# Two single-row blocks per turn instead of one in a GRU over gathered table rows: the second split between SyncE and ScalarE's queue, in a ring of 16 steps

## What is computed

```python
x = emb[item_seq]; mask = item_seq != 0          # 12,500 items x 128; sequences 512 x 200
def step(h, (x_t, m_t)):
    mx = x_t @ W + b_i
    mh = h @ U + b_r
    z = sigmoid(mx[:, :D] + mh[:, :D])
    r = sigmoid(mx[:, D:2*D] + mh[:, D:2*D])
    hh = tanh(mx[:, 2*D:] + r * mh[:, 2*D:])
    h_new = z * h + (1 - z) * hh
    return where(m_t, h_new, h)
out = softmax(h_last @ Wout + bout)
```

## Time and profile before

| what | value |
|---|---|
| median of 3 runs | 1039.23 us (1037.85 to 1040.12) |
| the profiled execution, its own time | 1038.45 us |
| its span, first to last instruction | 1036.5 us |
| busy share of the span | PE 94%, DVE 76%, POOL 74%, ACT 57% |
| granted TensorE clock, mean | 0.995 of full speed |
| DMA | 184.29 MB, mean 178 GB/s |
| chain that ended last | PE 55%, POOL 27%, "issue" 10%, DMA 3%, DVE 3%, ACT 1% |

### The profile page before, as it was taken

The page is one execution under the profiler, slowest core; times in us unless marked ns, Lnnn a source line. Parts: engine busy times, 40 slices in busy tenths (PEclk is TensorE's granted clock), DMA queues, the critical chain, the costliest instruction groups (busy, mean ns, idle before and its releaser), DMA issues.

```text
span 1036.5 us, 20050 instructions
## 1 busy us (share of the span) xinstructions
PE 976.5 (94%) x5218; PEld 760.8 (73%) x5218; DVE 792.0 (76%) x2075; ACT 593.2 (57%) x1301; POOL 765.7 (74%) x807
## 2 busy tenths in 40 slices
PE   6999999999999999999999999998898888988986
PEld 4556888777777777777777777776666666766765
DVE  3444667888888888888888888887777877777776
ACT  2334555666666666666666666655555555555555
POOL 5677777777777777777777777777777777777773
PEclk9999999999999999999999999999999999999999
DMA  9997555555555555555555555555555555555553
GB/s 356 403 373 279 150 161 159 161 161 160 163 158 161 163 157 161 161 161 161 159 163 158 161 160 161 160 160 162 157 161 163 157 160 161 159 161 159 164 163 95
DMA packets 62053, 184.29 MB, mean 178 GB/s; under 512 B 16428, under 2 KB 19812, under 8 KB 62020
## 3 DMA queue, kind: packets, MB, share of 16 engines
q0 software_dynamic: 48640, 147.77, 49.6%
q1 hardware_dynamic: 11984, 35.24, 8.9%
q10 hardware_dynamic: 1396, 0.91, 0.3%
HBM read 157.78 MB, written 26.07 MB: 177 GB/s over the span
## 4 chain that ended last, share of the span: by engine, by line
PE 55%; POOL 27%; issue 10%; DMA 3%; DVE 3%; ACT 1%; DVEq 0%; SPq 0%; POOLq 0%; ACTq 0%
POOL arena L359 27%; PE bank L453 14%; PE bank L459 9%; PE bank L455 9%; PE bank L441 8%; PE bank L375 5%; PE bank L447 4%; DMA rows<-turned 2%; PE bank L422 1%; PE bank L427 1%; PE bank L423 1%; DVE h L630 1%; ACT cand L561 1%; DVE rh L625 1%; PE bank L380 1%
## 5 line engine op out<-in xcount | busy, mean ns | idle before, releaser
L359 POOL DMA_INDIRECT arena<-table,row_table x734 | 694.7, 946 | 223.9 <-issue 218.7
L559 ACT ACTIVATE bank<-bank,b_gates 128x256 f32<-128x256 f32 x400 | 179.2, 448 | 252.2 <-PE bank L459 252.2
L441 PE MATMUL bank<-ident,arena 128*128 128x128 f32 x1496 | 249.8, 277 | 40.4 <-DMA arena<-table,row_table 39.5
L453 PE MATMUL bank<-h,U_sb 128*128 128x256 f32 x800 | 265.9, 414 | 1.7 <-DVE h L630 1.6
L640 DVE SCALAR_TENSOR_TENSOR bank<-bank,cand 128x256 f32<-128x256 f32 x400 | 172.7, 432 | 121.7 <-ACT cand L561 118.9
L441 PEld LDWEIGHTS bank<-ident,arena 128*128 128x128 f32 x1496 | 184.5, 141 | 106.0 <-DMA arena<-table,row_table 67.8
L561 ACT ACTIVATE cand<-pre,bi 128x256 f32<-128x256 f32 x400 | 202.9, 507 | 86.4 <-DVE pre L634 86.4
L459 PE MATMUL bank<-h,U_sb 128*128 128x256 f32 x800 | 240.3, 382 | 0.0
L625 DVE SCALAR_TENSOR_TENSOR rh<-bank,br,r 128x256 f32<-128x256 f32 x400 | 193.5, 484 | 58.2 <-ACT r L557 55.2
L455 PE MATMUL bank<-h,U_sb 128*128 128x256 f32 x800 | 237.9, 379 | 0.0
L557 ACT ACTIVATE r<-bank,b_gates 128x256 f32<-128x256 f32 x400 | 189.8, 475 | 34.2 <-PE bank L453 30.7
(11 more groups left out here) (61 smaller groups left out, 249.9 us busy)
## 6 DMA issues: line engine op xcount, KB each, us to landing
arena<-table SPq DMA_DIRECT2D x1792, 1.5 KB
table<-proj SPq DMA_DIRECT2D x24, 768.0 KB, 5.3
arena<-table,row_table POOLq DMA_INDIRECT x734, 3.1
arena<-in_L_rec_emb SPq DMA_DIRECT2D x12, 512.0 KB, 10.4
rows<-turned SPq DMA_DIRECT2D x12, 512.0 KB, 10.3
raw<-rows,row_table POOLq DMA_INDIRECT x52, 4.8
seq<-in_r_item_seq ACTq DMA_DIRECT2D x1, 400.0 KB, 10.5
table<-proj SPq DMA_DIRECT2D x2, 192.0 KB
```

The lines of the kernel that those rows point to most:

```text
L359: pool.indirect_dma_start(ring_rows(s, k), None, table, bass.IndirectOffsetOnAxis(row_table[:, t, k:k + 1], 0)).then_inc(s_slot[s][k], 16)
L441: pe.matmul(dst[:, i * P:(i + 1) * P], ring_row(s, k, g), ident[:, :], start=(i == 0), stop=False, is_transpose=True, skip_group_check=True)
L453: pe.matmul(reset_sum[c], U_sb[:, D:2 * D], h[c][:, :], start=False, stop=True, skip_group_check=True).then_inc(s_reset[c], 1)
L559: act.activation(update_sum[c], update_sum[c], ACT.Sigmoid, bias=b_gates[:, 0:1]).then_inc(s_z[c], 1)
```

## The change

A second block of each turn, slot (SHARED_STEP, SLOW_BLOCK) = (3, 3), is also fetched by single-row DMAs. SP issues its first 56 rows, in the turn before it is used. ScalarE's queue issues the other 72, at the turn's steps 4 to 15, one behind each of the six activations of a step; before the even ones of these twelve steps ACT loads 12 offsets into registers. SP's own block moves to slot (9, 3). The ring grows to 16 slots, so there are TURNS = 11 full turns and LEFT = 11 steps, 12 turns in all; the tiles `proj` move into the ring's last four slots. For the first turn SP fetches all 128 rows of both blocks.

```diff
-RING = 14
-SLOW_STEP = 4
+RING = 16
+SLOW_STEP = 9
+SHARED_STEP = 3
 SLOW_BLOCK = 3
 BATCH_ROWS = 32
+ACT_ROWS = 72
+ACT_STEPS = 12
...
+    SP_ROWS = P - ACT_ROWS
+    SLOW = ((SLOW_STEP, SLOW_BLOCK), (SHARED_STEP, SLOW_BLOCK))
...
-        proj = [sb(f"proj{q}", [P, GROUP, GATES]) for q in range(AHEAD)]
+        proj = [arena[:, (RING - AHEAD + q) * BLOCKS * GATES:][:, 0:GROUP * GATES].rearrange(
+            "p (j n) -> p j n", j=GROUP) for q in range(AHEAD)]
...
+        def load_offsets(eng, b, turn, first, n):
+            return nc.values_load_multi_w_load_instructions(
+                slow_line[b:b + 1, bass.ds(turn * P + first, n)], engines=[eng.engine],
+                min_val=0, max_val=(ITEMS + P) * ROW_BYTES,
+                skip_runtime_bounds_check_because="row numbers are clamped where they are made")[1]
+
+        def fetch_row(eng, b, p, offset):
+            return eng.dma_start(ring_rows(*SLOW[b])[p:p + 1, :].bitcast(U8),
+                                 table_bytes[:, bass.ds(offset, ROW_BYTES)])
...
-            sp.dma_start(slow_line[:, :], slow_turned[:, :]).then_inc(s_slow_line, 16)
+            for b in range(len(SLOW)):
+                sp.dma_start(slow_line[b:b + 1, :], slow_turned[b * (TURNS + 1):(b + 1) * (TURNS + 1), :]
+                             ).then_inc(s_slow_line, 16)
...
+            def fetch_rows(b, turn, first, n, signal):
+                offset = load_offsets(sp, b, turn, first, n)
+                for i in range(n):
+                    fetch_row(sp, b, first + i, offset[i]).then_inc(signal, 16)
 
             def slow_block(turn):
                 for first in range(0, P, BATCH_ROWS):
...
+                    fetch_rows(0, turn, first, BATCH_ROWS, s_slow)
+
+            fetch_rows(1, 0, 0, 32, s_shared_sp)
+            fetch_rows(1, 0, 32, SP_ROWS - 32, s_shared_sp)
+            fetch_rows(1, 0, SP_ROWS, 32, s_shared_act)
+            fetch_rows(1, 0, SP_ROWS + 32, 32, s_shared_act)
+            fetch_rows(1, 0, SP_ROWS + 64, ACT_ROWS - 64, s_shared_act)
             slow_block(0)
             with sp.Fori(1, TURNS + 1) as turn:
+
+                sp.wait_ge(s_free[1], (turn - 1) * RING + SHARED_STEP + 1)
+                fetch_rows(1, turn, 0, 32, s_shared_sp)
+                fetch_rows(1, turn, 32, SP_ROWS - 32, s_shared_sp)
+                sp.wait_ge(s_free[1], (turn - 1) * RING + SLOW_STEP + 1)
                 slow_block(turn)
...
-                        if (s, k) == (SLOW_STEP, SLOW_BLOCK):
+                        if (s, k) in SLOW:
                             continue
...
-                        if n == 0 and (s, k) == (SLOW_STEP, SLOW_BLOCK):
+                        if n == 0 and (s, k) == SLOW[0]:
                             pe.wait_ge(s_slow, (turn + 1) * (P * 16))
+                        elif n == 0 and (s, k) == SLOW[1]:
+                            pe.wait_ge(s_shared_sp, (turn + 1) * (SP_ROWS * 16))
+                            pe.wait_ge(s_shared_act, (turn + 1) * (ACT_ROWS * 16))
...
             def one_turn(turn, steps):
+                offset = []
                 for s in range(steps):
                     t = RAW + turn * RING + s
+
+
+                    i = s - SHARED_STEP - 1
+                    fetches = steps == RING and 0 <= i < ACT_STEPS
+
+                    def fetch(j):
+                        if fetches:
+                            fetch_row(act, 1, SP_ROWS + 6 * i + j, offset[6 * (i % 2) + j]).then_inc(s_shared_act, 16)
+
                     for c in BOTH:
-                        gates(t, c)
-
+                        reset(t, c)
+                        if fetches and c == 0 and i % 2 == 0:
+                            offset = load_offsets(act, 1, turn + 1, SP_ROWS + 6 * i, 12)
+                            if i == 0:
+                                act.wait_ge(s_free[1], turn * RING + SHARED_STEP + 1)
+                        fetch(3 * c)
+                        update(t, c)
+                        fetch(3 * c + 1)
+                        candidate(t, c)
+                        fetch(3 * c + 2)
+
+            act.wait_ge(s_slow_line, 16 * len(SLOW))
+            for q in range(AHEAD):
+                act.wait_ge(s_store[q], 16 * table_stores(q))
+            act.wait_ge(s_padrow, 16 * 2)
             over_table_steps(act, one_turn)
```

More of the change, by code:

```diff
@@ L53, in gru @@
     LEFT = STEPS - RAW - TURNS * RING
-    assert SLOW_STEP < min(RAW, LEFT)
+    SP_ROWS = P - ACT_ROWS
+    SLOW = ((SLOW_STEP, SLOW_BLOCK), (SHARED_STEP, SLOW_BLOCK))
+    assert SHARED_STEP < SLOW_STEP < LEFT and SHARED_STEP + ACT_STEPS < RING and ACT_ROWS == 6 * ACT_STEPS
     BOTH = range(len(CHAINS))
@@ L88, in gru @@
         turned_last = sb("turned_last", [P, 3, D])
-        proj = [sb(f"proj{q}", [P, GROUP, GATES]) for q in range(AHEAD)]
+        assert GROUP <= BLOCKS and ITEMS <= (RING - AHEAD) * BLOCKS * GATES
+        proj = [arena[:, (RING - AHEAD + q) * BLOCKS * GATES:][:, 0:GROUP * GATES].rearrange(
+            "p (j n) -> p j n", j=GROUP) for q in range(AHEAD)]
         def ring_row(s, k, g):
@@ L111, in gru @@
         row_table = sb("row_table", [P, STEPS, BLOCKS], I32)
-        slow_offsets = sb("slow_offsets", [P, TURNS + 1])
-        slow_turned = sb("slow_turned", [TURNS + 1, P], I32)
-        slow_line = sb("slow_line", [1, (TURNS + 1) * P], I32)
+        slow_offsets = sb("slow_offsets", [P, len(SLOW) * (TURNS + 1)])
+        slow_turned = sb("slow_turned", [len(SLOW) * (TURNS + 1), P], I32)
+        slow_line = sb("slow_line", [len(SLOW), (TURNS + 1) * P], I32)
         copy_i = sb("copy_i", [P, 1], I32)
@@ L181, in gru @@
         s_slow = sem("slow_rows_fetched")
+        s_shared_sp = sem("shared_first_rows_fetched")
+        s_shared_act = sem("shared_last_rows_fetched")
         s_x = per_chain("x_turned")
@@ L257, in _ @@
             sp.wait_ge(s_padrow, 16 * 2)
-            sp.wait_ge(s_slow_line, 16)
-            slot = ring_rows(SLOW_STEP, SLOW_BLOCK).bitcast(U8)
+            sp.wait_ge(s_slow_line, 16 * len(SLOW))
+            def fetch_rows(b, turn, first, n, signal):
+                offset = load_offsets(sp, b, turn, first, n)
+                for i in range(n):
+                    fetch_row(sp, b, first + i, offset[i]).then_inc(signal, 16)
             def slow_block(turn):
                 for first in range(0, P, BATCH_ROWS):
[L263 to L276, removed]
+                    fetch_rows(0, turn, first, BATCH_ROWS, s_slow)
[4 more added lines that the diff above has]
+            fetch_rows(1, 0, SP_ROWS + 64, ACT_ROWS - 64, s_shared_act)
             slow_block(0)
             with sp.Fori(1, TURNS + 1) as turn:
+                sp.wait_ge(s_free[1], (turn - 1) * RING + SHARED_STEP + 1)
+                fetch_rows(1, turn, 0, 32, s_shared_sp)
+                fetch_rows(1, turn, 32, SP_ROWS - 32, s_shared_sp)
+                sp.wait_ge(s_free[1], (turn - 1) * RING + SLOW_STEP + 1)
                 slow_block(turn)
@@ L326, in _ @@
             pool.wait_ge(s_idx, 7)
-            pool.tensor_scalar(slow_offsets[:, :], row_f[:, SLOW_BLOCK, RAW + SLOW_STEP:STEPS:RING],
-                               float(ROW_BYTES), None, ALU.mult).then_inc(s_offsets, 1)
+            for b, (s, k) in enumerate(SLOW):
+                pool.tensor_scalar(slow_offsets[:, b * (TURNS + 1):(b + 1) * (TURNS + 1)],
+                                   row_f[:, k, RAW + s:STEPS:RING], float(ROW_BYTES), None, ALU.mult
+                                   ).then_inc(s_offsets, 1)
             pool.tensor_copy(row_table[:, :, :], row_f.rearrange("p k t -> p t k")).then_inc(s_idx, 1)
             pool.wait_ge(s_idx, 8)
-            pool.wait_ge(s_offsets, 1)
+            pool.wait_ge(s_offsets, len(SLOW))
             pool.wait_ge(s_pins, 2)
@@ L402, in _ @@
                 project(i)
-            slow_bank = bank[1][0:TURNS + 1, 0:P]
-            pe.wait_ge(s_offsets, 1)
+            slow_bank = bank[1][0:len(SLOW) * (TURNS + 1), 0:P]
+            pe.wait_ge(s_offsets, len(SLOW))
             pe.wait_ge(s_tdve, CHUNKS + 1)
@@ L553, in turned_x, with reset, update, candidate @@
                 act.copy(xT[c][:, :], x_sum[c]).then_inc(s_xT[c], 1)
-            def gates(t, c):
+            def reset(t, c):
                 act.wait_ge(s_reset[c], t + 1)
                 act.activation(r[c][:, :], reset_sum[c], ACT.Sigmoid, bias=b_gates[:, 1:2]).then_inc(s_r[c], 1)
+            def update(t, c):
                 act.wait_ge(s_update[c], t + 1)
                 act.activation(update_sum[c], update_sum[c], ACT.Sigmoid, bias=b_gates[:, 0:1]).then_inc(s_z[c], 1)
+            def candidate(t, c):
                 act.wait_ge(s_pre[c], t + 1)
                 act.activation(cand[c][:, :], pre[c][:, :], ACT.Tanh, bias=bi[:, 2:3]).then_inc(s_tanh[c], 1)
+            def gates(t, c):
+                reset(t, c)
+                update(t, c)
+                candidate(t, c)
             for t in range(RAW):
@@ L571, in one_turn @@
```

(14 more changed lines are left out.)

2 lines of the change are left out of this document (1 added, 1 removed).

## The result

The changed kernel takes 1056.12 us (4 runs, 1054.51 to 1057.97) against 1039.67 (4 runs): a ratio of 1.0155, interval 1.0135 to 1.0175. It is slower by 1.55%, where 1025.8 us and a gain had been forecast. The profiled execution has a span of 1054.9 us.

What follows compares the result with a forecast made beforehand. POOL's gathers were taken to bound the end. Ten fewer gave net -13.4 us, SP's and ACT's added work was hidden: span 1023.1, plus 1.95 around it and 0.8 to the median, 1025.8 us; range 1023 to 1045.

Steps and rivals of the forecast that it cites:

- term 2: SP's queue: 72.4 us a turn, last row issued at 997 us, in time and so hidden.
- 9 us that were free: SP's queue at the end: last row due by 1006.4 us, expected at 997, so 9 us to spare.
- Term 1: POOL's gathers, taken as the bound: 724 instead of 734, the end net 13.4 us earlier.
- Rival (c): ACT's fetch behind the candidate, or the descriptor generator's lock on SP, makes it slower: 1042 to 1060 us; chance 0.12.
- Rival (a): SP's queue, held up 12 to 29 ns by each ACT DMA, becomes the bound: 1028 to 1037 us; chance 0.17.
- Term 3: ACT's queue: fetches cost nothing, each load makes the candidate 0.1 us late, 0.6 us a turn, hidden.
- x - 0.94: Gate chain on ACT: how late the candidate comes, in us, when a register load takes x.
- 2.4 us that were free: Gate chain's slack per turn: 26.6 us over 11 turns before it would delay the end.
- The estimate of 1.14 us: ACT's load of 12 offsets: 0.6 us floor plus 12/32 of the remaining 1.44; candidate late by 0.2.

Runs made afterwards that it cites:

- e3: The changed kernel with ACT's fetches and loads left out after the first turn: 1053.69 us in a single run.
- e1: The changed kernel with SP's eleven turns written out instead of looped: 1023.25 us, ratio 0.9845 to the kernel before.
- e2: The kernel before the change with two turns in each iteration of SP's loop: 1039.29 us in a single run, beside 1039.54.
- e10: The changed kernel with two turns in each of five iterations of SP's loop, the eleventh written out: 1034.38 us, ratio 0.9951.
- e4: The changed kernel with SP's turns written out, 78 shared rows by ACT in thirteen steps and 50 by SP: 1170.95 us, ratio 1.1265.

## Why the prediction was wrong

**The step that failed** is in term 2: "The new turn has 184 rows and 6 loads: 58.9 + 13.5 = 72.4 us", together with "The loop over fewer turns ... cost nothing". It priced rows and loads and gave the loop around them no price, though its body grew from 267 to 384 instructions. SP's last row was put at 98.6 + 102.2 + 796.4 = 997.2 us and came 41.3 us later. Added up over SP's queue, the ten jumps are 28.9 of it. The 37 pauses of 0.33 to 0.39 us, one each 128 instructions, are 11.4 beyond the usual gaps (the old loop had none after its first pass). ACT's part is 4.6 (row DMAs of 228.7 ns on the mean, 226.7 in e3, on 2,280 rows), the loop's own register and branch instructions 3.0, and the later start 1.3. That is 49.2; the rows and loads themselves took 7.9 less than 0.32 and 2.25 us each, mostly because the thirteen loads of 24 or 8 values are shorter than those of 32. Experiments e1, e2 and e10 show the jump's part. With the pauses and ACT's part alone, SP would still have kept nearly to its time: e1 has both, and SP's last row is 7.5 us late there, within the 9 us that were free.

**Term 1 (POOL) was right.** 724 gathers, 1.25 us apart, and where SP keeps up (e1) a span of 1021.4 against the 1023.1 of the sum. The last gather that PE waited for landed in 3.2 us there, where 4.06 had been put in.

**The slack was seen, not weighed.** The prediction said that SP's cover of 166 us of waits was gone and 9 us were left over 11 turns. It then asked only what ACT could do to those 9 us. The like question for SP's own program was not asked, and there 2.7 us a turn was enough. That rival was missing. Rival (c), 1042 to 1060, holds the measured 1056 for another reason (ACT's fetches late, or over 29 ns on SP for each): that it fits is luck.

**Rival (a) named the right bound with the wrong mechanism.** SP did become the bound. But ACT's DMAs cost SP 5.5 ns each, inside the 0 to 10 ns read from the earlier trace rows, where the rival needed 12 to 29. If that is the wait for the descriptor generator, it is small, as those rows had shown.

**Term 3 was right in what it decided, low in size.** A fetch behind a candidate costs nothing: steps with fetches and no load take 4.36 us. A load of 12 took 0.96 us (forecast 1.0 to 1.1). Yet steps with a load take 0.2 to 0.4 us more (two of them 0.5), not 0.1. The timeline of the changed kernel's ACT about such a load (which runs from 237.10 to 238.06) shows the rest:

```profile
237.02 0.47 ACT L586 ACTIVATE r<-bank,b_gates 128x256 f32<-128x256 f32 x1
238.16 0.47 ACTq L232 DMA_DIRECT2D arena<-table  x1
238.68 0.45 ACT L590 ACTIVATE bank<-bank,b_gates 128x256 f32<-128x256 f32 x1 [1.19 <-PE bank L488]
238.75 0.23 ACTq L232 DMA_DIRECT2D arena<-table  x1
239.05 0.50 ACT L594 ACTIVATE cand<-pre,bi 128x256 f32<-128x256 f32 x1
```

The first DMA behind a load takes 0.47 us (0.46 to 0.55 over the 66), not 0.23. So a load is late by x - 0.70 and not x - 0.94, which gives 0.26 at 0.96 us, and 2.07 at the 2.77 us of e4, where 2.07 was measured. The gate chain's turn is 71.7 us: 1.7 of the 2.4 us that were free, not 0.6.

**The estimate of 1.14 us** for that load, from the floor of about 600 ns in the Trainium skill ("DMA: Bandwidth & Descriptors", Latency and other measured facts), is above the 0.96 measured. The Trainium skill also gives about 200 ns for a register ("Runtime: NRT & Kernel Launch", Instruction fetch mechanics), of registers loaded from HBM, where the offsets here lie in SBUF. The unaligned loads of e4 agree with it at 0.20 to 0.21; the aligned ones took about a quarter of it, 0.21 to 0.22 for four.

## What to carry to other kernels

When a queue's work per turn grows, count the instructions of its loop's body too, and put the jump back into the sum: on SP it went from 0.22 to about 2.9 us between 267 and 384 instructions, ten times on the path that set the end, and writing the loop out turned a loss of 1.55% into a gain of 1.55%. A queue whose waits have been used up is a bound in waiting; then every fixed cost in its program counts, not only its DMAs. Start register loads at a multiple of four values, as the fast ones here did.

## What the runs showed of the hardware that was not expected

- **The jump back** took 0.2 us with up to two block boundaries in the loop and 2.4 to 3.5 us with three or more (bodies of 102 to 766 instructions); the boundaries stand 128 instructions apart. By that spacing the loop's place in the program decides between 258 and 384 instructions; seen it was at 276, 316 and 336.
- **Straight code pauses** 0.33 to 0.39 us at each block boundary on SP (every 61 row fetches or so), which a short loop does not after its first pass.
- **A register load** that starts at a multiple of four values takes 0.21 to 0.22 us more for each four; started two behind a multiple of four, 0.20 to 0.21 us for each value: 0.96 against 2.77 us for twelve.
- **The first DMA behind a load on ACT** takes 0.47 us, later ones 0.23.
- **A single row lands** 1.4 us after its issue (the last one above), where 3.1 us from POOL's gather had been put in.
- **PE's clock fell about most of the waits for SP's rows.** The changed kernel's stretches up to SP's last row and behind it, and inside the latter (busy us of PE, PEld, DVE, ACT and POOL, then PEclk):

```profile
1000.00:1038.00 38.00, 36.66 (x202) 28.95 (x201) 32.06 (x87) 23.44 (x52) 9.47 (x10) 1.00 0.22 63
1038.00:1055.00 17.00, 9.85 (x50) 8.15 (x50) 8.38 (x23) 6.93 (x18) 0.00 (x0) 0.80 0.05 13
1041.30:1044.70 3.40, 3.40 (x12) 2.72 (x11) 2.00 (x5) 1.39 (x4) 0.00 (x0) 0.50 0.02 5
```

The granted clock is 1.00 ahead of the wait, and 0.50, the lower of the two levels (1.2 GHz), from 1041.3 to 1044.7 us, behind a wait that ended at 1040.0. A pair of matmuls takes 0.86 us there (L488 at 1041.56) and 0.60 us at 2.4 GHz. ACT's r shows what it costs:

```profile
1040.87 0.48 ACT L586 ACTIVATE r<-bank,b_gates 128x256 f32<-128x256 f32 x1 [2.90 <-PE bank L482]
1044.16 0.47 ACT L586 ACTIVATE r<-bank,b_gates 128x256 f32<-128x256 f32 x1 [0.84 <-PE bank L482]
1046.54 0.47 ACT L586 ACTIVATE r<-bank,b_gates 128x256 f32<-128x256 f32 x1
```

They stand 3.29 and 2.38 us apart, where 2.18 is usual: 1.3 us in all. In e3, whose last wait no such stretch followed, they keep to 2.18, and SP's last row is 14.9 us before the end instead of 16.4. Seven of the changed kernel's eight waits have a stretch at 1.2 GHz beside them; the one that ended at 735.7 has none. The six ahead of the last cost the end nothing, since SP, which sets it, does not wait for PE.
